# Cross-attention with split float32 products: the 28 loads of Wo's operands issued from ScalarE's queue instead of SyncE's

## The reference, cut to what matters

```python
# x: (8, 1024, 1024), ctx: (8, 64, 1024), all float32, 16 heads of 64
a = layer_norm(ctx, gamma, beta)
Q = heads(x @ Wq.T); K = heads(a @ Wk.T); V = heads(a @ Wv.T)
attn = softmax(where(mask, (Q @ K.T) / 8, -inf))
return x + tanh(gate) * (unheads(attn @ V) @ Wo.T)
```

## Time and profile before

| | |
|---|---|
| time, median of 3 runs | 1497.65 us (1497.6 to 1498.21) |
| the profiled execution, its own time | 1495.54 us |
| its span in the trace | 1493.8 us |
| TensorE busy | 1470.4 us, 98% |
| VectorE busy | 1162.5 us, 78% |
| ScalarE busy | 894.2 us, 60% |
| GpSimd busy | 538.0 us, 36% |
| moved by DMA | 348.51 MB, 233 GB/s over the span |
| on SyncE's queue (q1) | 332.54 MB |
| on ScalarE's queue (q10) | 14.68 MB |

### The profile page before, as it was taken

The page is one execution under the profiler, slowest core; times in us unless marked ns, Lnnn a source line. Parts: engine busy times, 40 slices in busy tenths (PEclk is TensorE's granted clock), DMA queues, the critical chain, the costliest instruction groups (busy, mean ns, idle before and its releaser), DMA issues.

```text
span 1493.8 us, 20135 instructions
## 1 busy us (share of the span) xinstructions
PE 1470.4 (98%) x6624; PEld 1196.4 (80%) x6624; DVE 1162.5 (78%) x1349; ACT 894.2 (60%) x1894; POOL 538.0 (36%) x364
## 2 busy tenths in 40 slices
PE   6999999999999999999999999999999999999999
PEld 5666788888888888888787788888888888888887
DVE  6445888787878787879867678888888888888743
ACT  4556645454545555555776677766777776677521
POOL 5334000000000000000123576677766667776640
PEclk9999999999999999999999999999999999999999
DMA  7699865666565657464579988788988888888632
GB/s 278 221 382 390 304 217 189 211 212 211 190 225 184 232 182 233 170 224 157 161 247 313 297 252 243 229 253 245 265 262 244 228 244 249 243 265 266 210 120 84
DMA packets 303144, 348.51 MB, mean 233 GB/s; under 512 B 35648, under 2 KB 177088, under 8 KB 303040
## 3 DMA queue, kind: packets, MB, share of 16 engines
q1 hardware_dynamic: 287808, 332.54, 70.2%
q10 hardware_dynamic: 15232, 14.68, 2.8%
HBM read 198.26 MB, written 145.75 MB: 230 GB/s over the span
## 4 chain that ended last, share of the span: by engine, by line
PE 91%; DVE 3%; DMA 2%; issue 1%; SPq 1%; ACT 1%; POOL 0%; DVEq 0%; POOLq 0%; ACTq 0%
PE banks L1181 29%; PE banks L1182 29%; PE banks L1183 29%; PE banks L1210 3%; SPq L473 1%; DVE parts L973 1%; DMA s_scratch<-c_out 1%; DMA b_raw<-m_stage 1%; PE banks L1249 0%; DVE b_raw L993 0%; DVE a_ring L967 0%; DMA b_raw<-m_scratch 0%; DMA c_out<-x 0%; PE banks L1175 0%; DVE a_sum L1037 0%
## 5 line engine op out<-in xcount | busy, mean ns | idle before, releaser
L1181 PE MATMUL banks<-parts,a_ring 128*128 128x512 f32 x1792 | 700.6, 391 | 1.4 <-DVE a_ring L967 0.8
L1182 PE MATMUL banks<-parts,a_ring 128*128 128x512 f32 x1792 | 698.2, 390 | 0.0
L1183 PE MATMUL banks<-parts,a_ring 128*128 128x512 f32 x1792 | 698.1, 390 | 0.0
L1181 PEld LDWEIGHTS banks<-parts,a_ring 128*128 128x128 f32 x1792 | 337.1, 188 | 73.3 <-DVE a_ring L967 3.1
L1183 PEld LDWEIGHTS banks<-parts,a_ring 128*128 128x128 f32 x1792 | 337.0, 188 | 70.4
L1182 PEld LDWEIGHTS banks<-parts,a_ring 128*128 128x128 f32 x1792 | 337.2, 188 | 69.5
L967 DVE TENSOR_TENSOR a_ring<-a_sum,a_ring 128x1024 fp32r<-128x1024 f32 x128 | 225.1, 1758 | 79.0 <-ACT a_ring L738 79.0
L738 ACT CAST a_ring<-a_sum 128x1024 fp32r<-128x1024 f32 x128 | 134.3, 1049 | 234.2 <-PE banks L1183 205.3
L1059 DVE TENSOR_TENSOR c_out<-banks,c_out 128x1024 f32<-128x1024 f32 x159 | 193.3, 1216 | 102.9 <-PE banks L1183 99.3
L808 ACT ACTIVATE probs<-probs,neg_max 128x64 f32<-128x64 f32 x1024 | 258.7, 338 | 1.2 <-DVE neg_max L1073 1.2
L647 POOL TENSOR_TENSOR probs<-probs,row_rec 128x512 f32<-128x512 f32 x128 | 135.9, 1062 | 240.7 <-DVE row_rec L1082 240.7
(11 more groups left out here) (76 smaller groups left out, 1309.4 us busy)
## 6 DMA issues: line engine op xcount, KB each, us to landing
xq<-x_t SPq DMA_DIRECT2D x32, 1024.0 KB, 6.0
s_scratch<-c_out SPq DMA_DIRECT2D x64, 512.0 KB, 3.1
probs<-s_scratch SPq DMA_DIRECT2D x128, 256.0 KB, 4.1
c_out<-x SPq DMA_DIRECT2D x64, 512.0 KB, 5.4
out<-c_out SPq DMA_DIRECT2D x63, 512.0 KB, 4.3
b_raw<-m_scratch SPq DMA_DIRECT2D x29, 1024.0 KB, 6.7
m_scratch<-m_stage SPq DMA_DIRECT2D x16, 1792.0 KB, 13.3
p_scratch<-p_turned SPq DMA_DIRECT2D x448, 64.0 KB, 2.6
```

What stands on the lines that cost most here:

```text
L1181: pe.matmul(to, wl, mh, start=first, stop=False, skip_group_check=joined)
L1182: pe.matmul(to, wh, ml, start=False, stop=False, skip_group_check=joined)
L1183: return pe.matmul(to, wh, mh, start=False, stop=last, skip_group_check=joined)
```

## The change

The function load_wo_part moves from the SyncE program to the ScalarE program, with the same waits, addresses and semaphores. ScalarE calls it in steps 106 to 112, for k = s - 106: pieces 0 and 1 ahead of the work of the step's first slot, pieces 2 and 3 ahead of that of its second. SyncE issues none.

```diff
@@ SyncE
-            def load_wo_part(k, c):
-                if c == 0:
-                    sp.wait_ge(item_done, 2 * (14 * (B - 1) + 7 + k + 1))
-                if k == 0 and c == 0:
-                    for i in range(3):
-                        sp.wait_ge(wo_split_stored[i], 16 * ((WO_PIECES + 2 - i) // 3))
-                sp.dma_start(parts[:, k, :, c, :].bitcast(F32), wo_scr[k, :, :, c, :]).then_inc(wo_part_in[k], 16)
...
             for z in range(2 * STEPS):
                 slot(z)
-                for i in range(28):
-                    if 2 * (14 * (B - 1) + 8) + (18 * i // 28) == z:
-                        load_wo_part(i // 4, i % 4)
@@ ScalarE
+            def load_wo_part(k, c):
+                if c == 0:
+                    act.wait_ge(item_done, 2 * (14 * (B - 1) + 7 + k + 1))
+                if k == 0 and c == 0:
+                    for i in range(3):
+                        act.wait_ge(wo_split_stored[i], 16 * ((WO_PIECES + 2 - i) // 3))
+                nc.scalar.dma_start(parts[:, k, :, c, :].bitcast(F32), wo_scr[k, :, :, c, :]).then_inc(wo_part_in[k], 16)
...
                 for z in (2 * s, 2 * s + 1):
+                    k = s - 14 * (B - 1) - 8
+                    if 0 <= k < 7:
+                        for c in range(2 * (z % 2), 2 * (z % 2) + 2):
+                            load_wo_part(k, c)
                     for u in units(split_slot, z):
                         split_p_hi(u)
                     for u in units(evac_slot, z):
```

## The result

The changed kernel takes 1501.70 us (median of 14 runs, 1499.11 to 1504.22) against 1497.78 us for the kernel before on the same chip (14 runs): ratio 1.0025, with a 95% interval of 1.0018 to 1.0032. It is 3.9 us slower, outside the forecast's range, where 1491.4 had been forecast. The profiled execution took 1503.05 us (span 1501.3), 7.5 more than the profiled one of before.

A forecast was written before the change was run, and what follows sets the result against it. TensorE was taken as the bound, busy nearly throughout, with only two pauses to give back. 2.0 + 4.15 and a little made 6.3 us: 1495.5 - 6.3 = 1489.2, 1491.4 on the median; range from half a us under 1489.0 to 1497.6.

The forecast's parts named there:

- pause A: TensorE's stop on VectorE's p_parts, 801.38 to 807.70 us in the kernel before; priced at 4.5 us lost.
- pause B: TensorE's stop on GpSimd's p_parts for unit 16, 831.85 to 838.50 us in the kernel before; priced at 4.15 us lost.
- Items 1 and 2: 28 issues leave SyncE's queue and loads come earlier; unit 16's fetch comes sooner and pause B goes, worth 4.15 us.
- the sum: 2.0 us at pause A plus 4.15 at pause B, and a little for shorter VectorE waits: 6.3 us gained.
- Rival 2: Pause B stays because something else in SyncE's order holds the fetch; gain 0 to 2.5 us; chance 0.19.
- Item 3: ScalarE's queue takes 28 issues without new waits: at most 8.4 us against 12.0 free; step 112's exponentials 1.0 us late.
- Rival 3: ScalarE's queue fills and blocks it; some 7 us slower, 1504, or about 1500 with six issues blocked; chance 0.13.
- Item 4: c_out's store and load together take at most 11.5 us (13.45 before); net 2.0 us at pause A, bounds 0 to 4.5.
- Rival 1: Engines are full, c_out's store and load stay slow, pause A stays; gain 0.2 + 4.15 us, 1493.3; chance 0.16.

The follow-up runs named there:

- e3: The kernel before without the 28 Wo loads and the waits for them, so rounds 16 to 31 multiply by old data; 1493.00 us, ratio 0.9968.
- e7: Against the kernel before: SyncE issues two Wo loads in each slot 212 to 221, the last eight in 227 to 230; 1503.32 us, ratio 1.0030.
- e12: Against the kernel before: SyncE issues the Wo loads in rows of 4 KB, none in slots 221 to 223; 1498.87 us, ratio 0.9993.
- e10: The changed kernel with its 28 Wo loads cut into 1024 rows of 512 bytes instead of 256 of 2 KB; 1510.40 us, ratio 1.0083 against before.
- e2: The kernel before with SyncE still issuing the Wo loads, but two in each of slots 212 to 225; 1499.28 us, ratio 1.0008.
- e1: Against the kernel before: ScalarE issues the 28 Wo loads, in the slots of before (212 to 229); 1502.00 us, ratio 1.0024.
- e9: The changed kernel with its 28 Wo loads in 128 rows of 4 KB instead of 256 of 2 KB; 1501.95 us, ratio 1.0024 against before.

## Why the prediction was wrong

**The bounds and the two pauses.** Read rightly as causes: without the Wo loads (e3) pause A is 0.7 us and pause B gone. Their sum as a ceiling was wrong: 8.65 us were to be had, e3 shows 4.8. Waits of about 1 us on a_ring and GpSimd's p_parts, between 838 and 856 us, come forward where no long pause stands between 820 and 850 us; in the trace of before, with pause B at 834, only 0.35 us of them shows (at 847.68), in e7 none and in e12 0.15.

**Items 1 and 2, SyncE's issues and pause B.** Right. SyncE after the transpositions of unit 15:

```profile
828.11 0.36 SPq L466 DMA_DIRECT2D probs<-s_scratch  x1
828.52 1.95 SPq L473 DMA_DIRECT2D p_scratch<-p_turned  x4
...
836.06 0.39 SPq L485 DMA_DIRECT2D p_by_key<-p_scratch  x1
```

Four issues take 1.95 us and not 2.83, the fetch of unit 16 comes 7.95 us after the first issue (forecast 6.7, before 10.5), and TensorE doesn't wait. The 4.15 us were gained, though 1.9 went back to the small waits behind 840 us, which the sum put at nothing. Rival 2 is out.

**Item 3, ScalarE.** Right, and too careful: up to 8.4 us of idle time were allowed, the rows show 0.26 us for all 28. Rival 3 didn't occur; e10 shows that its mechanism exists.

**Item 4, the step that failed.** It took the store and load to be done within 11.5 us, since no more than two or three Wo loads can stand ahead of them, and on another queue. They took 14.20 + 6.38 = 20.6 us. Two things were wrong in that sentence. First, a transfer on the other queue isn't out of the way: it shares the engines with the short ones, and from 783.8 to 797 us ScalarE adds eight loads, where SyncE had added five. Neither half of the change makes the pair as slow as both do (e2 15.7 us, e1 15.8). Second, the share isn't even: rows of 512 B against 2 KB, as e9 and e10 show. Moreover the step looked at the pair alone. The loads of scores pass the same way, with 7.8 to 11.9 us for 4.0 to 7.3. Their delay stands in no term of the sum, and it made the new pause at 794.81 and had a part in the one at 812.99. Instead of 2.0 us gained at pause A some 7.0 us were lost there: 4.1 at 794.81 and 2.9 at 812.99 (7.4 less the 4.5 of before).

**Rival 1** had half of the mechanism, full engines, and the wrong price. It let the transfers remain as slow as they were, 8.3 us for the store and 13.45 for the pair, because it thought of the engines' total rate. The full engines are in the trace (share 1.06 and 380 GB/s in 780 to 800 us), but a total says nothing on who is served, and the pair took 20.6. The forecast gave this rival 0.16, and even it forecast a gain.

**The sum** as it was and as it came, on the profiled executions: pause A +2.0 forecast, -7.0 measured; pause B +4.15 forecast, +4.15 measured, less 1.9 for the small waits (2.4 us for the 0.5 of before). That is 4.7 us lost, and 23 fewer starts say 5.3; the medians say 3.9.

## What to carry to other kernels

Before moving bulk loads to a second queue, list all short transfers of the first that something waits for: on one queue they pass behind what was issued ahead of them, on two they share full engines with the other queue as well, and the queue with longer rows is served more (shown here for rows of 512 B beside 2 and 4 KB). Freed issue slots are worth something only where the rows show the issuing engine late (here at one place of two); cheap for the new issuer isn't cheap for the old one's transfers. A ceiling read off as the sum of pauses should be tried by leaving the suspected work out: one such run here cut it from 8.65 to 4.8 us.

## What was not expected of the hardware

- The row length of one queue's loads sets the latency of another queue's: 8.5, 11.9 and 17.8 us at most for 256 KB of scores beside Wo rows of 512 B, 2 KB and 4 KB.
- The same 512 KB cost 444 to 482 ns to issue in 128 rows of 4 KB, 612 in 256 rows of 2 KB, and 1751 in 1024 rows of 512 B (medians of 28), where the engine that issues stood still for up to 6.43 us.
- 28 issues on ScalarE's queue, 0.63 us each in the median, cost ScalarE 0.26 us of idle time in all: they run beside the instruction that executes.
- Beside a queue with rows of 512 B the engines carried 290 to 316 GB/s at a full share, beside one with rows of 2 KB 344 to 380.
